# A decoder kernel on one Trainium2 core: the last stage moved into the drain of the layer stream, the first part reordered, and other instruction orders on every engine in the stream

## The reference

```python
x = x + rel_pos_attention(layernorm(x))          # 8 heads of 128, learned relative positions
x = x + cross_attention(ctx, layernorm(x), mask) # 8 heads of 16
x = x + local_transformer(layernorm(x))
# local_transformer, 6 layers, t = shift_tokens(x):
#   q, k, v = t @ Wqkv (16 heads of 64); q, k normalized, scaled, rotated
#   x = x + softmax(window of 32 and the one before) @ v @ Wo
#   x = x + (a * gelu(gate)) @ W2 + b2,  a, gate = LN(shift_tokens(x)) @ W1 + b1, inner 341
```

## Time and profile before

| | us |
|---|---|
| runs | 4160.75, 4165.05, 4166.41; median 4165.05 |
| profiled execution | 4162.11 |
| its span | 4160.3 |
| part 1 and set-up, up to the first centre matmul | 861.3 |
| 46 full bodies | 3202.44 |
| first drain body | 48.0 |
| from there to the last z | 31.2 |
| final stage behind the last z | 17.4 |

### The profile page before, as it was taken

The page is one execution under the profiler, slowest core; times in us unless marked ns, Lnnn a source line. Parts: engine busy times, 40 slices in busy tenths (PEclk is TensorE's granted clock), DMA queues, the critical chain, the costliest instruction groups (busy, mean ns, idle before and its releaser), DMA issues. The chain is left out here.

```text
span 4160.3 us, 101562 instructions
## 1 busy us (share of the span) xinstructions
PE 3836.9 (92%) x30384; PEld 3048.3 (73%) x30384; DVE 3480.1 (84%) x11903; ACT 3245.7 (78%) x11174; POOL 3089.8 (74%) x3387
## 2 busy tenths in 40 slices
PE   7888888799999999999999999999999999999997
PEld 5777776577777777777777777777777777777774
DVE  5666766698988898989898989888888888898884
ACT  1555555688888888888888888888888888888885
POOL 2333332688888888888888888888898888888883
PEclk9999999799999999999999999999999999999998
DMA  4222222000000000000000000000000000000000
GB/s 146 87 81 76 86 78 71 22 5 1 2 2 7 22 2 2 2 1 28 2 2 2 2 7 23 2 2 2 1 28 2 2 2 2 8 2 2 2 2 21
DMA packets 76216, 86.67 MB, mean 21 GB/s; under 512 B 13622, under 2 KB 69396, under 8 KB 74836
## 3 DMA queue, kind: packets, MB, share of 16 engines
q1 hardware_dynamic: 75732, 80.87, 6.0%
HBM read 45.33 MB, written 35.52 MB: 19 GB/s over the span
## 5 line engine op out<-in xcount | busy, mean ns | idle before, releaser
L1266 ACT ACTIVATE p<-p,mx 128x128 f32<-128x128 f32 x3072 | 1189.3, 392 | 0.6
L1427 POOL TENSOR_TENSOR rot<-own_crossed 128x512 f32<-128x512 f32 x768 | 987.5, 1286 | 0.0
L1422 POOL TENSOR_TENSOR p<-p,ri 128x512 f32<-128x512 f32 x768 | 800.6, 1042 | 215.0 <-DVE ri L1370 213.7
L1418 POOL TENSOR_TENSOR rot<-rot,rn 128x512 f32<-128x512 f32 x768 | 802.9, 1045 | 48.2 <-ACT rn L1234 0.4
L1326 DVE CUSTOM_DVE_ANT_0 p<-bank_pair,band_f 128x128 f32<-128x128 f32 x3072 | 705.2, 285 | 58.5 <-issue 52.0
L1266 ACT ACTIVATION_READ_ACCUMULATOR p<-p,mx 128x1 f32 x3072 | 588.8, 192 | 0.0
L453 PE MATMUL bank<-wqkv_hi,xs_lo 128*128 128x512 f32 x1152 | 534.5, 464 | 15.7 <-DVE gel L1311 10.1
L1335 DVE TENSOR_REDUCE ss<-sq 128x8 f32<-128x512 f32 x768 | 522.9, 681 | 28.6 <-ACT sq L1280 28.6
L1365 DVE COPY pTl<-bank 128x512 f32<-128x512 f32 x768 | 522.7, 681 | 2.5 <-PE bank L1123 2.4
L1354 DVE TENSOR_TENSOR own_crossed<-bank,rot_tab 128x512 f32<-128x512 f32 x768 | 523.2, 681 | 1.7
L1136 PE MATMUL bank<-ident,rot 128*128 128x128 f32 x3072 | 469.6, 276 | 48.1 <-POOL rot L1418 48.1
(11 more groups left out here) (198 smaller groups left out, 7358.3 us busy)
## 6 DMA issues: line engine op xcount, KB each, us to landing
pos_scratch<-pos_sb SPq DMA_DIRECT2D x32, 1020.0 KB, 4.3
sc<-pos_scratch SPq DMA_DIRECT2D x32, 512.0 KB, 4.0
wqkv_raw<-in_L_ffn_Wqkv SPq DMA_DIRECT2D x6, 1536.0 KB, 6.9
ctx_sb<-in_ctx SPq DMA_DIRECT2D x32, 128.0 KB, 3.5
wo<-in_L_ffn_Wo SPq DMA_DIRECT2D x6, 512.0 KB, 4.3
mrow<-in_mask_BxS_fk SPq DMA_DIRECT2D x1, 2048.0 KB, 7.7
x_all<-in_x SPq DMA_DIRECT2D x4, 512.0 KB, 8.8
out<-res SPq DMA_DIRECT2D x8, 256.0 KB, 2.3
```

The costliest lines, as they stand in the source:

```text
L1266: last = nc.scalar.activation(p[:, j, h, :], p[:, j, h, :], ACT.Exp, bias=mx[:, j, h:h + 1], scale=-1.0, accum_out=psums[:, j, h:h + 1])
L1418: nc.gpsimd.tensor_tensor(rot[:, (k - 8) % 4, :, :], rot[:, (k - 8) % 4, :, :], rn[:, (k - 8) // 2 % 4, (k - 8) % 2, :].unsqueeze(2).to_br ...
L1422: nc.gpsimd.tensor_tensor(p[:, j, :, :], p[:, j, :, :], ri[:, j, :].unsqueeze(2).to_broadcast([128, G, T]), ALU.mult).then_inc(L["pn"], 1)
L1427: nc.gpsimd.tensor_tensor(rot[:, (k - 7) % 4, :, :], own[:, (k - 7) % 4, :, :], crossed[:, (k - 7) % 4, :, :], ALU.add).then_inc(L["rot0"], 1)
```

## The change

1. **Final stage.** final_scalar, final_tensor and final_vector go. Their blocks stand at the end of a step in the stream's emit of ScalarE, TensorE and VectorE: quads 0 to 5 in steps 6 to 11 (ScalarE), 7 to 12 (TensorE) and 8 to 13 (VectorE) of the first drain body, quad 6 in steps 3, 4 and 5 of the last body, quad 7 in its step 15. final_sync stays.
2. **Part 1.** The next batch's xh is transposed into a slot of another bank between xh2's transpose and out2, once Y has been copied, and the rounded position matmuls of pairs 0 and 1 (four of eight) follow between q2 and S2. ScalarE does Y's copy before xh2T's and then the next batch's two copies of xh's transpose. VectorE's and GpSimd's code is unchanged.
3. **Stream.** V has delay 9 (7 before), v_sb too; p·ri 15 (14 before); the weight groups of V are renewed two steps later. FFN steps: var and rstd 4, gate 0 and 1 at 7, gate 2 at 9, value 1 at 10, value 0 at 11, value 2 at 12, y at 13, xg and xn_lo one step earlier. The new order within a step:
   - PE: gate2[9], S, var[4], gate0[7], value1[10], value0[11], PV, QK, V, value2[12], T2, centre[2], T1, WO, gate1[7], y[13], final
   - ACT: xs, xn[6], gelu1, gelu2 and table, exp, oT, ln/exp of the norms, rstd[4], v_sb, rounding of V's groups, sq, rounding of QK's, qkT, xsq/xcg[2], GELU table and gelu0[9], final
   - DVE: maxima, gate0[7], value0[11], gate1[8], reduce, tables, own, value2[12], crossed, value1[10], ri, gate2[8], z[14], pTl, res, biases, final
   - POOL: p·ri, rot, clamp, rot0, xg[5], xn_lo[6], xs_lo, weight halves

The diff, cut to its core (the moved blocks of the stream are the same text in the orders above):

```diff
--- before.py
+++ after.py
...
+        XH_T = banks[1][:, 0:128]
...
+            def pos_rounded(u, j, pairs):
+                for pr in pairs:
+                    for part, w in enumerate(C_w):
+                        nc.tensor.matmul(POS_PS[pr][:, 0:2 * NR], xhT_hi[:, j, :], w[:, 2 * pr:2 * pr + 2, :].rearrange("p h n -> p (h n)"),
+                                         start=(part == 0), stop=False)
+            def turn_next(u, j):
+                pe.wait_ge(S1["xh"], u + 1)
+                nc.tensor.transpose(XH_T, xh[:, j, :], ident[:, :]).then_inc(S1["xhT_mm"], 1)
...
-                if on(0):
-                    pe.wait_ge(S1["xh"], u0 + 1)
...
-                    nc.tensor.transpose(SMALL_T, xh[:, i0, :], ident[:, :]).then_inc(S1["xhT_mm"], 1)
...
                     pe.wait_ge(S1["xhT"], u0 + 1)
-                    if reused(first, k, 0, 1):
-                        pe.wait_ge(S1["summed"], u0)
-                    for pr in range(4):
-                        if pr == 2 and reused(first, k, 0, 1):
-                            pe.wait_ge(S1["Y"], u0)
-                        for j, w in enumerate(C_w):
-                            nc.tensor.matmul(POS_PS[pr][:, 0:2 * NR], xhT_hi[:, i0, :], w[:, 2 * pr:2 * pr + 2, :].rearrange("p h n -> p (h n)"),
-                                             start=(j == 0), stop=False)
+                    pos_rounded(u0, i0, (2, 3))
...
+                if on(-1):
+                    pe.wait_ge(S1["Y"], u0 + 1)
+                    turn_next(u0 + 1, (k + 1) % 2)
...
+                if on(-1):
+                    pe.wait_ge(S1["xhT_hi"], u0 + 2)
+                    pe.wait_ge(S1["summed"], u0 + 1)
+                    pos_rounded(u0 + 1, (k + 1) % 2, (0, 1))
...
-            pipeline(pe, B, 2, 3, emit, peeled=2)
+            turn_next(0, 0)
+            pe.wait_ge(S1["xhT_hi"], 1)
+            pos_rounded(0, 0, (0, 1))
+            pipeline(pe, B, 2, 3, emit, peeled=2, peeled_last=1)
...
         def part1_scalar(act):
+            def keep_next(u, j):
+                act.wait_ge(S1["xhT_mm"], u + 1)
+                nc.scalar.activation(xhT_hi[:, j, :], XH_T, ACT.Copy).then_inc(S1["xhT_hi"], 1)
+                nc.scalar.activation(xhT[:, j, :], XH_T, ACT.Copy).then_inc(S1["xhT"], 1)
...
+                if on(-1):
+                    if reused(first, k, -1, 2):
+                        act.wait_ge(S1["Y_mm"], u0)
+                    keep_next(u0 + 1, (k + 1) % 2)
+            keep_next(0, 0)
+            pipeline(act, B, 2, 3, emit, peeled=2, peeled_last=1)
...
+            def final_quad(self, d, k6):
+                if self.l < LAYERS - 1 or self.q < QUADS:
+                    return None
+                if self.q == QUADS:
+                    return self.k - d if 0 <= self.k - d < QUADS - 2 else None
+                return {k6: QUADS - 2, BODY - 1: QUADS - 1}.get(self.k)
...
                 if at.ffn(10):
                     if at.values_at(9):
-                        pe.wait_ge(L["v"], at.P + 2)
+                        pe.wait_ge(L["v"], at.P + 1)
                     else:
                         pe.wait_ge(Fm["gate"], 3 * at.F + 3)
+                    value(1)
+                if at.ffn(11):
+                    pe.wait_ge(Fm["u"], 3 * at.F + 1)
                     value(0)
-                if at.ffn(15):
...
+                if on(9) and k % 2 == 1:
...
+                    elif at.again(9, 2):
+                        pe.wait_ge(L["v"], at.pair(9))
...
+                if at.ffn(12):
+                    if at.values_at(11):
+                        pe.wait_ge(L["v"], at.P + 2)
+                    else:
+                        pe.wait_ge(Fm["u"], 3 * at.F + 2)
+                    value(2)
...
+                if on(18) and (k - 18) % UB == UB - 1:
...
+                    pe.wait_ge(L["oT"], at.pair(18) + 1)
+                    for c in range(OUT_CHUNKS):
+                        slot = (k - 18 - (UB - 1) + c // 2) % 8
+                        last = nc.tensor.matmul(y_ps, wo[:, c, :], oT[:, slot, c % 2 * T:(c % 2 + 1) * T], start=(c == 0), stop=(c == OUT_CHUNKS - 1))
+                    last.then_inc(L["WO"], 1)
...
+                f = at.final_quad(7, 4)
+                if f is not None:
+                    if f == 0:
+                        pe.wait_ge(L["own_crossed"], LAYERS * UNITS)
+                    pe.wait_ge(O["copied"], f + 1)
+                    if f >= 2:
+                        pe.wait_ge(O["added"], f - 1)
+                    for a in range(QUAD):
+                        last = nc.tensor.transpose(banks[f % 2][:, a * 128:(a + 1) * 128], zq[:, f % 2, a * 128:(a + 1) * 128], ident[:, :])
+                    last.then_inc(O["T_mm"], 1)
...
+                if at.ffn(4):
+                    act.wait_ge(Fm["var"], at.F + 1)
+                    nc.scalar.activation(rstd[:, :], ffn_ps[:, :], ACT.Ln, bias=eps_col[:, 0:1], scale=1.0).then_inc(Fm["log"], 1)
+                    act.wait_ge(Fm["log"], at.F + 1)
+                    nc.scalar.activation(rstd[:, :], rstd[:, :], ACT.Exp, scale=-0.5).then_inc(Fm["rstd"], 1)
+                if on(9) and k % 2 == 1:
...
+                    nc.scalar.activation(v_sb[:, (k - 9) % 16:(k - 9) % 16 + 2, :, :].rearrange("p u h n -> p (u h n)"), v_ps[:, :], ACT.Copy).then_inc(L["v"], 1)
...
+                if at.ffn(9):
+                    use_table(GELU_SET)
+                    gelu(0)
+                f = at.final_quad(6, 3)
+                if f is not None:
+                    act.wait_ge(L["z"], QUADS * LAYERS + f + 1)
+                    if f >= 2:
+                        act.wait_ge(O["T_mm"], f - 1)
+                    for rows, kept in kept_halves(f * QUAD, QUAD):
+                        last = nc.scalar.activation(zq[rows, f % 2, :].rearrange("p (a n) -> p a n", a=QUAD), kept, ACT.Copy)
+                    last.then_inc(O["copied"], 1)
...
+                if at.ffn(11):
+                    value(0, 1)
+                if at.ffn(8):
+                    keep_gate(1)
...
+                if at.ffn(12):
+                    value(2, 2)
...
+                if at.ffn(10):
+                    value(1, 0)
...
                 if at.ffn(8):
-                    keep_gate(1)
+                    keep_gate(2)
+                if at.ffn(14):
...
+                    last.then_inc(L["z"], 1)
...
+                f = at.final_quad(8, 5)
+                if f is not None:
+                    dve.wait_ge(O["T_mm"], f + 1)
+                    if f >= 2:
+                        dve.wait_ge(O_stored[f % 2], 16 * (f // 2))
+                    nc.vector.tensor_tensor(res[:, f % 2, :, :].rearrange("p a n -> p (a n)"), banks[f % 2][:, :],
+                                            x_all[:, f * QUAD:(f + 1) * QUAD, :].rearrange("p a n -> p (a n)"), ALU.add).then_inc(O["added"], 1)
...
+                if on(15):
+                    j = n(15) % 5
+                    wait_apart(pool, L["ri"], n(15) + 1)
+                    nc.gpsimd.tensor_tensor(p[:, j, :, :], p[:, j, :, :], ri[:, j, :].unsqueeze(2).to_broadcast([128, G, T]), ALU.mult).then_inc(L["pn"], 1)
...
+                if at.ffn(5):
+                    wait_apart(pool, Fm["rstd"], at.F + 1)
+                    nc.gpsimd.tensor_tensor(xg[:, :], xcg[:, :], rstd[:, :], ALU.mult).then_inc(Fm["xg"], 1)
```

More of the change, by code:

```diff
@@ L1065, in value @@
                     split_product(ffn_ps[0:m, :], [w[:, c0:c0 + m] for w in w1], [x[:, :] for x in xn]).then_inc(Fm["a"], 1)
[L1067 to L1071, removed]
-                    pe.wait_ge(Fm["xsq"], at.F + 1)
-                    nc.tensor.matmul(ffn_ps[:, :], mean_w[:, :], xsq[:, :], start=True, stop=True).then_inc(Fm["var"], 1)
+                if at.ffn(9):
+                    pe.wait_ge(Fm["gate"], 3 * at.F + 2)
+                    gate(2)
                 if on(10) and (k - 10) % 2 == 1:
@@ L1161, in emit @@
                                   [w[:, 0:2, g * G * DL:(g + 1) * G * DL] for w in wqkv]).then_inc(L["proj_qk"], 1)
-                if on(18) and (k - 18) % UB == UB - 1:
-                    if at.layer_start(1) and k == 5:
-                        pe.wait_ge(L["wo_in"], 16 * (l + 1))
-                    pe.wait_ge(L["oT"], at.pair(18) + 1)
-                    for c in range(OUT_CHUNKS):
-                        slot = (k - 18 - (UB - 1) + c // 2) % 8
-                        last = nc.tensor.matmul(y_ps, wo[:, c, :], oT[:, slot, c % 2 * T:(c % 2 + 1) * T], start=(c == 0), stop=(c == OUT_CHUNKS - 1))
-                    last.then_inc(L["WO"], 1)
-                if on(7) and k % 2 == 1:
+                if on(9) and k % 2 == 1:
                     if at.ffn(3):
@@ L1197, in emit @@
                     nc.tensor.matmul(ffn_ps.rearrange("p (a n) -> p a n", a=QUAD), centre_w[:, :], shifted(at.ffn_batch(), QUAD), start=True, stop=True).then_inc(Fm["centre"], 1)
-                if at.ffn(10):
-                    pe.wait_ge(Fm["u"], 3 * at.F + 1)
```

(34 more changed lines are left out.)

258 lines of the change are left out of this document (82 added, 176 removed).

## The result

The changed kernel takes 4093.24 us (median of 4 runs, 4086.93 to 4095.0) against 4164.8 in the same job: a ratio of 0.9825, 95% interval 0.9813 to 0.9836, or 71.6 us less. The forecast was 4075 with a range of 4005 to 4155. The profiled execution took 4086.93, its span is 4085.1, 75.2 less than the 4160.3 of before.

The account below looks back on a forecast made before the run. TensorE's rate was taken to bound the stream, through its waits and pitch. Stream −92, table stalls +15, part 1 −4, tail −11.3 and drain +2 gave −90: 4075 us against the median, range 4005 to 4155.

Parts of the forecast that it names:

- The floor: Stream: an ordinary body without waits, walked in the new order, takes 65.2 us, against 65.65 in the old order.
- 1.4 + 0.2: Stream: waits left in an ordinary body, 1.4 us for uf, maxima, v_sb and others, plus 0.2 for VectorE behind WO.
- Other queues: … nothing.: Stream: GpSimd's p times ri, one step later but first in its step, costs nothing; GpSimd isn't the bound.
- T1 stands late in TensorE's step, so rot is there in time: Stream: TensorE's transposes of rot, which waited 43.6 us for GpSimd, no longer wait.
- The late WO: Stream: WO, moved behind V, T2 and T1, comes 0.7 us later for VectorE; priced at 0.2 us a body.
- the first rival: Stream: WO comes too late for VectorE's res and maxima, body 70.8 us, kernel slower at 4244; chance 0.12.
- The table operation: Layer starts: GpSimd runs 11 us unbroken, each rot_tab stall grows by 0 to 5.5 us, 3 taken: +15 over five.
- It seems to finish when GpSimd next pauses: Layer starts: VectorE's rot_tab ends only at GpSimd's next pause; up to 8 us expected in the new order.
- Part 1: Part 1: TensorE's 19.3 us wait for xhT goes but becomes a longer wait for pos_sb; −4 us (−20 to +5).
- Drain and tail: End: tail −11.3 us (−10 to −12); first drain body +2 (0 to +6), copies hidden, partly paid on TensorE.
- the table stall in full: Layer starts: GpSimd without a pause at each layer, +27 us for the +15, kernel at 4087; chance 0.08.
- The slow loop: Stream: a four-step loop from S through WO and VectorE's maxima sets the pace at 17.7 us, 4244; chance 0.12.

Follow-up runs that it names:

- pool_old: The changed kernel with GpSimd's old order (p times ri at delay 14): 4158.82 us, 0.9983 of the kernel before.
- before_gelu_last: The kernel before with ScalarE's GELU table load and gelu of gate 0 moved to the end of step 9, behind v_sb: 4216.84 us, ratio 1.0121.
- the pause: The changed kernel with GpSimd waiting at each layer start for VectorE's rot_tab and rot_x, and later for its bias copies: 4039.46 us, 0.9709 of the kernel before.
- wo_early: The changed kernel with WO back behind QK and ahead of V on TensorE: 4331.59 us, 1.0398 of the kernel before.

## Why the prediction was right, and where it was not

**The ordinary body.** 66.85 measured for 66.8 forecast: 88 us less, more than the whole, since the rest together is a loss. But the sum was right by luck, by two errors that cancel. The floor was put at 65.2 and came out at 65.6, so the new order gives next to nothing in pitch: QK behind PV costs only 0.02 (1.02 from PV to QK, 0.34 to its second matmul for 0.32), but S, which now follows T1, starts 0.53 after it, where a product starts 0.36 after. That is 0.17 for each S and not 0.1. And the waits were put at 1.4 + 0.2 and are 1.2. The largest of them was foreseen in place and size, 0.73 idle for 0.9 with the pitch.

**"Other queues: … nothing."** This sentence priced GpSimd's new order at nothing, and it failed, with "T1 stands late in TensorE's step, so rot is there in time". The gain was put down to ScalarE's order. pool_old, with T1 as late, shows that without GpSimd's order 2.0 us a body are lost again to one wait for rot. And the opposite single step, ScalarE's late GELU alone, made the old kernel slower (before_gelu_last). So the gain can't be given to one engine. In the new kernel the old place of one block (WO) costs 238 us and GpSimd's old order 66; in the old kernel one block at its new place costs 50. Which of the other moved blocks matter stays open; they weren't tried one by one.

**The late WO.** It was priced at a loss of 0.2 a body, the first rival made more of it, and the experiment says the reverse: at its old place it costs 6.1. The walk followed what comes behind WO, res and the maxima, and left out what comes ahead of it: oT, for which WO itself waits, and V, which stands behind WO in TensorE's queue.

**The table operation.** The collision and the length of the run on GpSimd were right: 11 us forecast, 10.9 measured. The stall is 10.4 with rot_x for 5.4 at the median, 5.0 more where 3 was taken and 5.5 was the bound. It still cost only 12 us over the opening bodies for the 15. "It seems to finish when GpSimd next pauses" came true for rot_x and not for rot_tab, which was to take up to 8 us and took 1.2. What was missed is that the bias copies meet the same fate, 13 us in the bodies behind, since of VectorE's lines only rot_tab's was read the earlier trace rows. No term was given to the clock that falls behind a long wait. Here the Trainium skill could have warned: "SBUF — State Buffer", section "Who interferes with whom", counts copies among the operations that can take the shared pair. The runs agree with it there (0.16 with the pause for 2.8). For a wait of one GpSimd instruction, as that section's rule gives it, some 1.3 us here, they show both: rot_tab and the copy of 0.75 waited for the rest of one, rot_x through nine in a row. The measurement decides.

**Part 1.** −4 forecast; −7.4 between the two profiled executions, −11 in the mean over all traces, −3.8 by the times, whose intervals leave room for any of these. The term was taken too small. The wait did move to pos_sb, but the wait for q2T went with that for xhT, and the dips of the clock became fewer and shorter.

**Drain and tail.** The tail's 11.3 came out to the tenth. The drain's +2 was mis-sized: +5.4 here, near its upper bound of 6, and +8.9 in the old order. "Partly paid on TensorE" was too small. Of the 5.4 us, TensorE's own busy time is 4.5 (45.56 for 41.03, the transposes 3.8 of it), and its idle time is 0.9. The copies on ScalarE were nearly hidden here; in the old order they were not. The final stage's move is worth 5.9 us here and nothing that can be told in the old kernel.

**The sum.** 4075 for a measured 4093. Against the forecast the bodies behind the opening ones took 13 us more, the ordinary bodies 4 and the drain 3; part 1 took 3 less and the opening bodies 3. **Of the rivals**, the table stall in full came nearest with 4087, by luck: its +27 measured +12. The slow loop did not happen. Two orders that are slow, wo_early's and pool_old's, are slow by other waits, for oT and for rot.

## What to carry to other kernels

In a kernel whose engines hand over to each other every 3 us, read a reordering as one step: a block moved alone can cost as much as the whole brings. Where a rare VectorE operation with two SBUF inputs, or a copy from SBUF to SBUF, stands beside a GpSimd that never pauses, look at its longest duration beside its shortest; a wait that lets GpSimd stand idle for it took off 48 us in the two places, more than half as much as the whole change. When a wait of several us appears on TensorE, read the granted clock behind it too: the wait's price is both. A stage moved into a drain costs what it adds to the engine that the drain hangs on, here TensorE.

## What was not expected of the hardware

- A VectorE copy of 128x4 values, 0.16 us alone, took 2.82 beside a busy GpSimd, and an operation of 0.68 took 9.24, through nine GpSimd operations in a row. Yet rot_tab, the operation just ahead, got its turn behind one. GpSimd's large operations don't grow (rot takes 1.04 us inside that stretch and 1.07 ahead of it).
- With small extra work on TensorE in a stretch of long waits its granted clock there was 0.83 for 0.55, and the last body with the tail was 2.7 us shorter.
- One wait of 2.2 us in each body of pool_old was followed in some bodies by a stretch at a granted clock of 0.50 and in others not. It made 70.4 us of 68.9. Part 1 has the same in single steps, 2.4 us each in the kernel before.
